# A decoder layer on one core: the two changes of phase put in another order, SBUF tensors moved, and the last two cross-attention products summed in one bank

## The reference

```
x = x + self_attn(layernorm(x))        # 32 heads of 128, 8 key heads, 16 cached blocks of 32 keys + 128 new = 640 keys
x = x + cross_attn(layernorm(x), ctx)  # h = rmsnorm(.) * ln_weight; 32 heads of 128; 128 keys for each of the 8 tiles
                                       # scores + position_bias, masked, softmax; returns h_in + attn @ w_out.T
x = x + ffn(layernorm(x))              # gelu(h @ W1 + b1) @ W2, non-finite -> 0, + b2; 512 -> 2048 -> 512
```

## Time and profile before

| | us |
|---|---|
| three runs | 2060.99, 2063.16, 2063.26; median 2063.16 |
| the profiled execution's own time | 2060.67 |
| span of its trace | 2058.9 |
| PE busy | 2029.4 (99% of the span), 11442 matmuls |
| DVE busy | 1373.5 (67%) |
| ACT busy | 1036.6 (50%) |
| POOL busy | 555.6 (27%) |

### The profile page before, as it was taken

One profiled execution on the slowest core, in us unless ns is written; L12 is line 12 of the kernel. 1 busy time (PEld: TensorE's weight loads), 2 busy tenths in 40 slices (PEclk: granted clock), 3 DMA queues, 4 the chain that ended last, 5 costly groups with the idle time before them and its releaser, 6 DMA issues.

```text
span 2058.9 us, 33150 instructions
## 1 busy us (share of the span) xinstructions
PE 2029.4 (99%) x11442; PEld 1755.4 (85%) x11442; DVE 1373.5 (67%) x2243; ACT 1036.6 (50%) x2272; POOL 555.6 (27%) x451
## 2 busy tenths in 40 slices
PE   8999999999999999999899999999999999998998
PEld 6888888888888888888788888888888888886887
DVE  7777777777777777777766666666666666667132
ACT  4555555555555555555544444444444444446443
POOL 3212212221222122212222222222222222213643
PEclk9999999999999999999999999999999999999999
DMA  7000000000000000011111101111111111002232
GB/s 242 19 18 21 21 11 20 20 20 10 20 20 20 10 20 20 15 47 41 40 53 44 36 35 43 43 43 43 43 43 43 43 43 43 24 22 72 89 116 77
DMA packets 48775, 85.36 MB, mean 41 GB/s; under 512 B 7890, under 2 KB 14162, under 8 KB 48210
## 3 DMA queue, kind: packets, MB, share of 16 engines
q1 hardware_dynamic: 48722, 84.64, 13.2%
HBM read 82.52 MB, written 2.10 MB: 41 GB/s over the span
## 4 chain that ended last, share of the span: by engine, by line
PE 94%; DVE 3%; ACT 2%; DMA 0%; issue 0%; SPq 0%; ACTq 0%; DVEq 0%
PE bank L1176 23%; PE bank L1178 23%; PE bank L1177 23%; PE bank L1245 11%; PE bank L1310 7%; PE bank L1378 1%; PE bank L1410 1%; PE bank L1379 1%; PE bank L1411 1%; PE bank L1420 1%; PE bank L1235 1%; DMA kv_raw<-in_wk 0%; DVE xacc L1135 0%; PE bank L1197 0%; ACT xn L495 0%
## 5 line engine op out<-in xcount | busy, mean ns | idle before, releaser
L897 DVE SCALAR_TENSOR_TENSOR xacc<-bank,rinv,xacc 128x512 f32<-128x512 f32 x504 | 370.2, 745 | 70.9 <-PE bank L1178 70.6
L478 ACT ACTIVATE pT_hi<-bank 128x512 fp32r<-128x512 f32 x320 | 190.9, 598 | 213.5 <-PE bank L1310 213.4
L887 DVE TENSOR_REDUCE negmax<-bank 128x1 f32<-128x640 f32 x256 | 210.3, 822 | 38.3 <-PE bank L1245 30.8
L953 DVE TENSOR_TENSOR pT_lo<-bank,pT_hi 128x512 fp32r<-128x512 f32 x320 | 217.9, 681 | 2.4 <-ACT pT_hi L478 2.4
L530 ACT ACTIVATE prob<-bank,negmax 128x640 f32<-128x640 f32 x256 | 202.6, 791 | 24.7 <-DVE negmax L887 24.7
L1310 PE MATMUL bank<-ident,prob 128*128 128x128 f32 x1280 | 191.2, 272 | 0.0
L1310 PEld LDWEIGHTS bank<-ident,prob 128*128 128x128 f32 x1280 | 159.2, 140 | 19.5
L383 POOL TENSOR_TENSOR wo_lo<-wo_raw,wo_hi 128x512 fp32r<-128x512 f32 x32 | 41.6, 1300 | 420.9 <-ACT wo_hi L478 420.9
L624 ACT ACTIVATE xprob<-xscore,negmax 128x128 f32<-128x128 f32 x256 | 99.5, 391 | 92.3 <-DVE negmax L1004 92.2
L1176 PE MATMUL bank<-xwv_hi,cT_hi 128*128 128x256 f32 x512 | 141.7, 277 | 1.4 <-DVE xV_lo L971 1.4
L1178 PE MATMUL bank<-xwv_hi,cT_lo 128*128 128x256 f32 x512 | 141.5, 276 | 0.0
(11 more groups left out here) (182 smaller groups left out, 5730.6 us busy)
## 6 DMA issues: line engine op xcount, KB each, us to landing
w_raw<-in_w SPq DMA_DIRECT2D x64, 256.0 KB, 2.8
wq_raw<-in_wq SPq DMA_DIRECT2D x32, 256.0 KB, 2.6
wo_raw<-in_wo SPq DMA_DIRECT2D x32, 256.0 KB, 2.6
xwv_raw<-in_xwv SPq DMA_DIRECT2D x16, 512.0 KB, 3.3
xwk_raw<-in_xwk SPq DMA_DIRECT2D x32, 256.0 KB, 3.6
xwq_raw<-in_xwq SPq DMA_DIRECT2D x32, 256.0 KB, 3.5
xwo_raw<-in_xwo SPq DMA_DIRECT2D x32, 256.0 KB, 2.7
xacc<-in_x SPq DMA_DIRECT2D x8, 256.0 KB, 6.3
```

The lines of the kernel that those rows point to most:

```text
L478: return s.activation(dst, src, ACT.Copy)
L887: v.tensor_reduce(negmax[:, slot, i:i + 1], S_bank[i % 2], mybir.AxisListType.XY, ALU.max, negate=True).then_inc(a["max"], 1)
L897: v.scalar_tensor_tensor(xacc[:, 4 * half + i, :], M, rinv[:, k, i:i + 1], xacc[:, 4 * half + i, :], ALU.mult, ALU.add).then_inc(sems["y"], 1)
L953: v.tensor_tensor(pT_lo[:, j, :], T_bank[j % 2 if k == 0 else (j + 1) % 2], pT_hi[:, j, :], ALU.subtract).then_inc(a["pTlo"], 1)
```

## The change

**Order of the middle passage.** On PE the two `spin` calls go; `values(0, 0)` stands ahead of the last `a_out`; the four `values` calls write banks 4, 6, 7, 6 (`V_first`) instead of bank 6 each; `values(1, 0)` stands ahead of the transposes of half 0, and `c_scores(0, 0)` ahead of those of half 1, whose four tiles take banks 2, 3, 7 and 5 in place of 0 to 3. On DVE the second layernorm is cut into `second_variance`, `second_centre`, `second_inner` and `second_outer`, and the last additions to `xacc` stand between them in two pairs; tiles 6 and 7 are scaled by DVE instead of ACT. ACT's calls are put in an order to match.

**Last two units.** `last_pv` makes 12 matmuls of 128 columns into one bank (`XO_last`) in place of 8 of 256, so the copy and the addition between product and rounding are dropped for these two units. For unit 63 it stands two `late_out` later than before, and its `row_factors` stand behind the third layernorm's `ln_lo`.

**Gelu table.** A one-element gelu is issued on ACT behind `ln_hi(3, 0)`, which has the table loaded there.

**Additions.** DVE's four additions of `last_o` had `h_lo(1)` behind them and `ln_stats(1)` ahead of `h_lo(2)`; now `h_lo(1)` stands behind the first addition and `h_lo(2)` ahead of `ln_stats(1)`.

**Places.** Seven allocations that nothing reads change the addresses: the self-attention's tensors from `K_all` to `idx_sb` lie 320 bytes higher, `prob`, `pT`, `oT` and `kv_raw` 768, `xwv` 1024, the FFN's weights 320, its other tensors 256 or 288. Those of the cross-attention (`cT`, `xwk`, `xwq`, `xk`, `xV`, `xwo`, `xpT`) stay.

```diff
+            sb(ph, "shift1", [P, 80])
             K_all = sb(ph, "K_all", [P, KB, NKV, BLOCK])
...
+            sb(ph, "shift5", [P, 112])
...
+                sb(lo_, "ahead3", [P, 64])
                 xwv_raw = sb(lo_, "xwv_raw", [P, C, 2 * P])
...
+            sb(ph, "shift6", [P, 80])
             w1_raw = sb(ph, "w1_raw", [P, 2, C, P])
...
-            sb(ph, "shift4", [P, 122])
+            sb(ph, "shift4", [P, 106])
...
+        XO_last = bank[:, 3, :]
+        V_first = [bank[:, i, :] for i in (4, 6, 7, 6)]
         def ln_bank(p, b):
+            if p == 2 and b >= 4:
+                return (2, 3, 7, 5)[b - 4]
             return LN3_bank[b] if p == 3 else b % 4
...                                             ACT, middle
+            v_evac(0, 0, 1, V_first[0])
             ln_sqrt(2, 1)
-            v_evac(0, 0, 1)
             ln_sqrt(2, 2)
-            v_evac(0, 1, 2)
-            ln_scale(0)
+            v_evac(0, 1, 2, V_first[1])
             k_evac(0, 0, 1)
-            ln_hi(2, 0)
+            ln_scale(0, range(4))
+            ln_hi(2, 0, (0, 1))
+            v_evac(1, 0, 3, V_first[2])
+            ln_hi(2, 0, (2, 3))
+            k_evac(1, 1, 2)
             residual(0)
-            v_evac(1, 0, 3)
             ln_sqrt(2, 3)
-            k_evac(1, 1, 2)
+            xq_evac(0, 0, 1)
+            v_evac(1, 1, 4, V_first[3])
             ln_sqrt(2, 4)
-            ln_scale(1)
-            xq_evac(0, 0, 1)
-            v_evac(1, 1, 4)
+            ln_scale(1, (4, 5))
             ln_hi(2, 1)
             c_exps(0, 0)
...                                             ACT, end
+            act.wait_ge(L[3, "sqrt"], 1)
+            s.activation(warm[:, :], nrm[:, 1, 0:1], ACT.Gelu_apprx_tanh)
             act.wait_ge(s_b1, 16 * NF)
             gelu(0)
...                                             DVE, middle
+            second_variance(0)
             dve.wait_ge(s_lnw, 16)
-            layernorm(2, xn2, 0, meanwhile=lambda: v_evac(0, 0, 1))
+            second_centre(0)
+            v_evac(0, 0, 1, V_first[0])
+            second_inner(0)
+            last_attention((0, 1))
+            second_outer(0).then_inc(s_factor, 1)
+            last_attention((2, 3))
+            v_evac(0, 1, 2, V_first[1])
+            xk_lo_evac(0, 1)
             dve.wait_ge(a["y"], LAST1)
             ln_stats(1)
-            v_evac(0, 1, 2)
-            xk_lo_evac(0, 1)
+            second_variance(1)
             ln_lo(2, 0)
-            v_evac(1, 0, 3)
-            layernorm(2, xn2, 1, meanwhile=lambda: xk_lo_evac(1, 2))
+            second_centre(1)
+            second_inner(1)
             xq_lo_evac(0, 1)
+            v_evac(1, 0, 3, V_first[2])
+            xk_lo_evac(1, 2)
+            second_outer(1).then_inc(s_factor, 1)
+            dve.wait_ge(s_factor, 2)
+            for b in (6, 7):
+                v.tensor_scalar(xn2[:, b, :], xn2[:, b, :], nrm[:, 6, b:b + 1], None, ALU.mult).then_inc(s_xnv, 1)
+            v_evac(1, 1, 4, V_first[3])
             ln_lo(2, 1)
...                                             DVE, end
-            h_lo(0)
             dve.wait_ge(c["y"], LAST1 - 4)
+            dve.wait_ge(s_lasto, 4)
             for i in range(4):
-                dve.wait_ge(s_lasto, i + 1)
+                if i < 2:
+                    h_lo(i)
                 v.tensor_tensor(xacc[:, 4 + i, :], last_o[:, i, :], xacc[:, 4 + i, :], ALU.add).then_inc(c["y"], 1)
-            h_lo(1)
+            h_lo(2)
...                                             PE, middle
-            spin(5, 12)
             pe.wait_ge(s_clo, C)
             pe.wait_ge(c["vwlo"], 1)
-            values(0, 0, 0)
-            values(0, 1, 1)
+            values(0, 0, None, V_first[0])
+            pe.wait_ge(a["oTlo"], UNITS)
+            for i in range(4):
+                a_out(UNITS - 1, 1, i, bank[:, i, :])
+            values(0, 1, None, V_first[1])
             c_keys(0, 0, 0)
+            pe.wait_ge(a["y"], LAST1 - 4)
+            values(1, 0, None, V_first[2])
+            pe.wait_ge(a["y"], LAST1)
             ln_transpose(2, xn2, 0)
-            values(1, 0, 2)
             pe.wait_ge(c["klo"], 1)
             c_keys(0, 0, 1)
             pe.wait_ge(L[2, "lo"], 4)
+            pe.wait_ge(c["vlo"], 1)
             c_queries(0, 0, 0)
-            values(1, 1, 3)
+            values(1, 1, 2, V_first[3])
+            c_scores(0, 0)
             ln_transpose(2, xn2, 1)
-            spin(7, 14)
             pe.wait_ge(L[2, "lo"], B)
-            c_scores(0, 0)
-            pe.wait_ge(c["qlo"], 1)
             c_queries(0, 0, 1)
...                                             PE, end
+            def last_pv(n, hp):
+                pe.wait_ge(c["pTlo"], n + 1)
+                for i in range(4):
+                    cols, dst = slice(hp * P, (hp + 1) * P), XO_last[:, i * P:(i + 1) * P]
+                    t.matmul(dst, xV_hi[:, 1, i, cols], xpT[:, i, 0], start=True, stop=False)
+                    t.matmul(dst, xV_hi[:, 1, i, cols], xpT[:, i, 1], start=False, stop=False)
+                    last = t.matmul(dst, xV_lo[:, 1, i, cols], xpT[:, i, 0], start=False, stop=True)
+                last.then_inc(c["pv"], 1)
...
-            late_out(n - 1, 0, XW_last)
-            c_pv(n, 1, 1)
-            for i in range(1, 4):
+            for i in range(4):
+                if i == 2:
+                    last_pv(n, 1)
                 pe.wait_ge(c["y"], 4 * (n - 2) + i + 1)
                 late_out(n - 1, i, XW_last)
```

More of the change, by code:

```diff
@@ L489, in ln_hi, with ln_scale @@
                          bank[:, ln_bank(p, b), :].rearrange("p (c n) -> p c n", c=C)).then_inc(L[p, "hi"], 1)
-            def ln_scale(half):
-                for b in range(4 * half, 4 * half + 4):
+            def ln_scale(half, tiles):
+                for b in tiles:
                     act.wait_ge(s_xl, b + 1)
@@ L791, in layernorm @@
                 sl = slice(4 * half, 4 * half + 4)
-                cnt = (2 if p == 2 else 1) * half
                 for b in range(4 * half, 4 * half + 4):
@@ L965, in _, with last_attention, v_evac @@
             ln_stats(0)
-            for i in range(4):
-                accumulate(a, UNITS - 1, 1, 1, i, bank[:, i, :], None)
-            def v_evac(half, j, cnt):
+            out_lo(UNITS)
+            def last_attention(tiles):
+                for i in tiles:
+                    accumulate(a, UNITS - 1, 1, 1, i, bank[:, i, :], None)
+            def v_evac(half, j, cnt, src=XV_bank):
                 dve.wait_ge(c["vhi"], cnt)
-                v.tensor_tensor(xV_lo[:, half, 2 * j:2 * j + 2, :], XV_bank.rearrange("p (t n) -> p t n", t=2),
+                v.tensor_tensor(xV_lo[:, half, 2 * j:2 * j + 2, :], src.rearrange("p (t n) -> p t n", t=2),
                                 xV_hi[:, half, 2 * j:2 * j + 2, :], ALU.subtract).then_inc(c["vlo"], 1)
@@ L981, in xk_lo_evac, with second_variance @@
                                 ALU.subtract).then_inc(c["klo"], 1)
-            dve.wait_ge(s_lnw, 16)
-            layernorm(2, xn2, 0, meanwhile=lambda: v_evac(0, 0, 1))
+            def second_variance(half):
+                for b in range(4 * half, 4 * half + 4):
+                    last = v.bn_aggr(meanvar[:, b, :], stats[:, b, :])
+                link(last)
+                sl = slice(4 * half, 4 * half + 4)
+                v.tensor_scalar(nrm[:, 0, sl], meanvar[:, sl, 1], EPS, None, ALU.add).then_inc(L[2, "stat"], 1)
@@ L1125, in _ @@
             ln_lo(3, 0)
+            row_factors(UNITS - 1)
             dve.wait_ge(c["rinv"], UNITS)
@@ L1146, in _ @@
             for n in range(2, FUNITS):
-                h_lo(n)
+                if n > 2:
+                    h_lo(n)
                 if n == 2:
@@ L1190, in ln_transpose @@
                 for b in tiles or range(4 * half, 4 * half + 4):
-                    pe.wait_ge(L[p, "xn"], b + 1)
+                    if p == 2 and b >= 6:
+                        pe.wait_ge(s_xnv, b - 5)
+                    else:
+                        pe.wait_ge(L[p, "xn"], b + 1)
                     if p < 3 and b >= 4:
@@ L1344, in _, with values @@
             pv(UNITS - 1, 1, 1, KT - 1, 7, 7)
-            pe.wait_ge(a["oTlo"], UNITS)
-            for i in range(4):
-                a_out(UNITS - 1, 1, i, bank[:, i, :])
             cT = (cT_hi, cT_lo)
-            def values(half, j, cnt):
-                if not isinstance(cnt, int) or cnt > 0:
+            def values(half, j, cnt, dst=XV_bank):
+                if cnt is not None:
                     pe.wait_ge(c["vlo"], cnt)
```

87 lines of the change are left out of this document (41 added, 46 removed).

## The result

The changed kernel takes 2045.5 us (median of four runs, 2041.91 to 2046.31) against 2062.36 for the kernel before (four runs): a ratio of 0.9915, interval 0.9898 to 0.9933. That is 17 us, where the sum had 10.1 and the forecast was 2053 within 2044 to 2058.

The account below looks back on a forecast made before the run. PE was taken to bound both attention loops, being busy throughout. Middle 7.0, end 3.1 and places 0 sum to 10.1 us; from the three-run median of 2063.16 that gives 2053, range 2044 to 2058.

Parts of the forecast that it names:

- the sum: Whole kernel: gains of 7.0 in the middle passage, 3.1 at the end and 0 from places, together 10.1 us.
- The places: Moved tensors' addresses, over 6000 matmuls in self-attention and FFN: bounds of 5 us either way, taken as nothing.
- places make matmuls faster: Rival: moved tensors lose 2.5 ns a matmul in two to four thousand, 5 to 10 us more, 2043 to 2048; chance 0.18.
- The middle: Passage between self-attention and cross-attention loops: the new order without spins gains 7.0 us, from 5.5 to 8.
- both 1.41 us waits: Middle passage: PE's waits for the low part of `oT` and for the bank's evacuation before the second `values`, both to go.
- laid out: Middle passage: PE's new list priced from the last product's end at 981.4, with scores done at about 1007.
- 0.2 off: Middle passage: POOL's `comb` additions delay DVE by up to 2 us near 987, mostly in slack; 0.2 taken off.
- The clock: Rival: without spins PE's clock falls in the middle, 1.8 us or double if both passages fall, 2055 to 2057; chance 0.13.
- The end: Last two products, gelu table and additions: a gain of 3.1 us, from 0 to 4.3.
- The wait at the fourth `y`: End, FFN: a new wait of about 1 us, since the list ahead of `h_lo(3)` starts 2.5 us earlier, PE 4.
- spreading the additions: End: only one addition ahead of `h_lo(1)`, so the second `y`'s 1.58 us wait goes, a gain of 1.6.
- I had 2.1: End: running gain of 2.1 us, from the first `hidden` 1.3 earlier and some 0.8 more by the early gelu table.

## Why the prediction was right, and where it was not

The direction and the range held, and so did the removed waits and spins of both passages. The median, 2045.5, lies 7.5 under the forecast of 2053, near the low end. What the forecast summed, the order without the places, was measured at 2052.76. That it comes so near is in part luck: the sum of 10.1 compares with 8.8, and the base of 2063.16 with 2061.56 beside that run.

**The places were the term that was mis-sized.** I had allowed 5 us either way and taken nothing, "since the rows don't say which property of the tensors makes the sort". The rows didn't, and that part stands; but what was there could have carried more. The earlier trace rows shows 2.77 and 2.80 us where, by the changed kernel, 2.72 was to be had, and I took the faster of the two sorts as the best possible. The term was 8.1 us, from the runs with places alone: 4.6 us in the self-attention's loop (4.8 with the weights alone) and 3.2 in the FFN. The rival "places make matmuls faster" with its 5 to 10 us, 2043 to 2048, is what happened, and had a chance of 0.18. Its mechanism, 2.5 ns less in some two to four thousand matmuls, was only roughly right: in the FFN `hidden` won 3 ns a matmul and `y` 7, in the self-attention the queries 2 (2.06 to 2.04 us for nine) and the output projection nothing (0.78 us for three in either kernel). The Trainium skill, "SBUF — State Buffer", section "Who interferes with whom", by whose sentence that PE and ACT never wait on anyone the places would give nothing, doesn't cover this: the distance of PE's matmuls did follow the addresses (2.72, 2.76, 2.80 us for the same twelve), in a kernel of which nothing else differed.

**The middle, forecast 7.0 (5.5 to 8): 5.5, and 6.5 with the clock held.** Both spins and both 1.41 us waits went, and the scores were done 26.8 us after the last product, 0.9 later than laid out. The difference is the wait of 1.26 us at 996.83, which I hadn't seen: DVE's list kept up less well than assumed. One cause is a term that I had priced too low. DVE and POOL of the changed kernel:

```profile
983.46 0.64 DVE L788 TENSOR_TENSOR nrm<-nrm 128x4 f32<-128x4 f32 x1
984.14 1.21 DVE L789 TENSOR_TENSOR nrm<-nrm 128x4 f32<-128x4 f32 x1
982.79 2.54 POOL L428 TENSOR_TENSOR comb<-bias_sb,negmask 128x512 f32<-128x512 f32 x2 [2.70 <-issue]
```

Two operations on four columns, 0.16 us each elsewhere, took 1.85 together while POOL made `comb`: 1.5 us of delay, where I took 0.2 off, with "most of it in slack". DVE has no idle time from there to the wait at 996.83, so the delay isn't in slack; that the whole 1.26 us comes from it is argued, since no run moved `comb` alone. The slowed ones have two inputs in SBUF; the reciprocal ahead of them, with one, took its 0.16 us beside POOL too.

**The clock.** It fell in the passage that the rival named, behind the wait of 2.00 us ahead of the last transposes: the 16 transposes took 3.38 us instead of 2.50, and the clock was 0.66 from 1005 to 1010; and it fell at the end as well. Priced from the start of the kernel at 1.8 us each, the two falls cost 1.0 and 1.6. I gave it 0.13, on the ground that in before a stretch from 1863 to 1873 with the same kind of gaps had stayed at 1.00. That was one execution: the kernel with the places alone, with just these gaps, fell to 0.81. A clock that held once is weak evidence that it holds. Nor was the fall something that the change brings: 18 of 28 executions of the kernel before show a clock of 0.997 or 0.998, and the base, a median of 2063.16, is of their size. The price of 2055 to 2057 most likely counted a loss that the base already held. The Trainium skill, "TensorE: Matmul & The Clock Gate", section "The HAM clock gate", says that the clock halves when the engine has been idle and returns after sustained work. The traces agree in that each fall seen in the two passages stands behind gaps of 1.2 to 2.0 us, and none was seen with the gaps filled; but behind the same gaps the clock stayed at 1.00 in the profiled execution of before.

**The end, forecast 3.1 (0 to 4.3): 2.97 with the clock held**, 1.6 in the profiled execution of the changed kernel. A 128-column product of twelve took 1848.79 - 1847.40 = 1.39 us, so 0.116 each, near the 0.108 taken, and the first `hidden`, with the table already loaded, ran into a first `y` without a wait. The wait at the fourth `y` was forecast at 1 us and is 1.40. But I had booked 1.6 us for spreading the additions, and then 1 us of new wait as a separate matter; the run with only the additions undone shows both to be one: the gain is 0.1. It is the last products, with the moved row factors, and the table that make the 3 us, some 2.9 where I had 2.1; the two were not undone one by one. That the whole came out at 3.1 against 2.97 is luck: one term 0.8 too small, the other 0.9 too large.

## What to carry to other kernels

When PE is busy throughout, look at the distance of its matmuls before believing that nothing is left: the same group of twelve at 2.72, 2.76 and 2.80 us differs by 3% (0.4% of the whole kernel here), and a few hundred bytes of padding decide it; but try each set of places on the chip, for the rule fitted to the FFN did not hold in the cross-attention. Put fillers where the gaps are: the kernel before had two and lost its clock at other gaps. And judge the clock by several executions, since one that kept it proves little; look at the granted clock of each run before comparing single times. When two steps of a sum are "this wait goes" and "a new wait comes behind it", ask first whether it is one queue and one wait.

## What was not expected of the hardware

That the addresses of operands in SBUF change how closely matmuls follow each other: 0.2267 us for 512 columns at best, 0.2333 in the `y` groups of before. That the value matmuls of 256 columns went from 2.72 to 2.82 us in 24, with their own two tensors unmoved. And that the same program keeps or loses its clock from one execution to the next, 8 times against 18 for the kernel before; with the gaps filled, four executions lay within 1.0 us instead of 4.4.
